# Batch 0's way through the setup of a fused 16-batch layer kernel: order of the first loads, q and k by halves of the heads, and who packs when

## The reference

```python
# 0: adapter with an expert chosen by domain_id, residual, layer norm
h = gelu(x @ down_W.T + down_b); h = (h @ expert_W[id].T + expert_b[id]) + domain_emb[id]
x = ln(h @ up_W.T + up_b + x) * gamma0 + beta0
# 1: attention, 16 heads of 16, modulated by the time step
scale, shift = split(silu(sin_emb(step)) @ W_ada + b_ada)
x1 = ln(x) * (1 + scale) + shift
s = (x1 @ Wq + bq) @ (x1 @ Wk + bk).T / 4 + attention_bias[b, h]      # per head
x = x1 + softmax(where(mask, -inf, s)) @ (x1 @ Wv + bv) @ Wo + bo
x = x + gelu2((ln(x) * g2 + beta2) @ W1 + b1) @ W2
# 2: one of three small networks by condition, residual, layer norm
# 3: finite differences of x times two grids, one time step, relu
```

## Time and profile before

| | |
|---|---|
| three runs | 863.94, 866.76, 868.88 us |
| profiled execution | 864.66 us, span 862.8 us |
| PE busy | 808.2 us (94%), 5968 matmuls |
| DVE, ACT, POOL busy | 738.2 (86%), 622.8 (72%), 164.7 us (19%) |
| TensorE's granted clock | 0.979 of full over the span |
| DMA | 137.33 MB, mean 159 GB/s; queue q1 (SP) 63.4% of 16 engines' span, q10 (ACT) 0.5% |
| chain that ended last | PE 83%, DVE 8%, SPq 3%, ACT 2% |
| side<-in_side | 128 DMAs of 512 KB, median 5.3 us to landing |

### The profile page before, as it was taken

How to read it: one execution, slowest core, us unless ns; L and a number is a source line. 1 busy time by engine, 2 the same in 40 slices (tenths; PEclk the granted TensorE clock), 3 DMA queues, 4 the chain that set the end, 5 groups by cost and what they waited for, 6 DMA issues and landing times.

```text
span 862.8 us, 18592 instructions
## 1 busy us (share of the span) xinstructions
PE 808.2 (94%) x5968; PEld 691.2 (80%) x5968; DVE 738.2 (86%) x2474; ACT 622.8 (72%) x1284; POOL 164.7 (19%) x160
## 2 busy tenths in 40 slices
PE   5686899999999999999999999999999999999992
PEld 2474598888888888888888888888888888887782
DVE  4766777898989899898989898998989898979687
ACT  2445787878778787878788787878788787677541
POOL 3210113030211222030211222030211222111020
PEclk9789999999999999999999999999999999999997
DMA  5866877575866777585767676585777758584100
GB/s 174 232 173 160 212 153 191 143 189 155 175 164 164 185 173 170 139 194 154 176 161 169 178 175 184 123 194 155 174 161 177 181 153 184 130 160 129 58 24 25
DMA packets 147609, 137.33 MB, mean 159 GB/s; under 512 B 19298, under 2 KB 144803, under 8 KB 147508
## 3 DMA queue, kind: packets, MB, share of 16 engines
q1 hardware_dynamic: 146548, 135.28, 63.4%
q10 hardware_dynamic: 960, 0.79, 0.5%
HBM read 98.23 MB, written 4.23 MB: 119 GB/s over the span
## 4 chain that ended last, share of the span: by engine, by line
PE 83%; DVE 8%; SPq 3%; issue 2%; ACT 2%; DMA 1%; ACTq 1%; POOL 0%; DVEq 0%; POOLq 0%
PE back_bank L1366 13%; PE turn_bank L1322 12%; PE context_bank L1376 7%; PE score_bank L1562 7%; PE score_bank L1563 6%; PE front_bank L1360 5%; PE attend_bank L1360 5%; PE back_bank L1360 5%; PE front_bank L1415 3%; PE back_bank L1346 3%; PE back_bank L1337 3%; PE attend_bank L1346 3%; PE front_bank L1668 2%; PE attend_bank L1307 2%; PE front_bank L1406 2%
## 5 line engine op out<-in xcount | busy, mean ns | idle before, releaser
L567 ACT ACTIVATE sc<-sc,negmax 128x256 f32<-128x256 f32 x512 | 231.3, 504 | 17.9 <-DVE negmax L1198 16.9
L1198 DVE CUSTOM_DVE_ANT_0 sc<-score_bank,side 128x256 f32<-128x256 f32 x512 | 195.2, 418 | 32.1 <-PE score_bank L1563 26.7
L561 ACT ACTIVATE pt<-turn_bank 128x512 f32<-128x512 f32 x176 | 106.2, 604 | 132.3 <-PE turn_bank L1322 106.6
L1322 PE MATMUL turn_bank<-ident,sc 128*128 128x128 f32 x1024 | 156.9, 276 | 1.1 <-ACT sc L567 1.0
L1322 PEld LDWEIGHTS turn_bank<-ident,sc 128*128 128x128 f32 x1024 | 123.5, 141 | 31.9 <-issue 14.1
L1562 PE MATMUL score_bank<-ks,qs 128*128 128x256 f32 x512 | 122.5, 321 | 4.3 <-issue 4.1
L1366 PE MATMUL back_bank<-w,ffT 128*128 128x256 f32 x512 | 118.5, 379 | 0.4 <-DVE ffT L1107 0.4
L1366 PEld LDWEIGHTS back_bank<-w,ffT 128*128 128x128 f32 x512 | 96.7, 190 | 13.5 <-DVE ffT L1107 1.0
L487 POOL TENSOR_TENSOR rstd<-var,half_neg 128x2 f32<-128x2 f32 x64 | 50.9, 796 | 285.8 <-DVE var L960 284.4
L1563 PE MATMUL score_bank<-mask_neg,ident_r 128*128 128x512 f32 x256 | 102.3, 400 | 0.0
L1562 PEld LDWEIGHTS score_bank<-ks,qs 128*128 128x128 f32 x512 | 78.2, 192 | 12.3 <-issue 10.9
(11 more groups left out here) (246 smaller groups left out, 1977.5 us busy)
## 6 DMA issues: line engine op xcount, KB each, us to landing
side<-in_side SPq DMA_DIRECT2D x128, 512.0 KB, 5.3
qs<-qh SPq DMA_DIRECT2D x128, 64.0 KB, 4.2
qs<-ql SPq DMA_DIRECT2D x128, 64.0 KB, 4.2
ks<-kl SPq DMA_DIRECT2D x124, 64.0 KB, 4.3
ks<-kh SPq DMA_DIRECT2D x120, 64.0 KB, 4.0
wb<-in_wb SPq DMA_DIRECT2D x15, 512.0 KB, 7.3
xN<-in_x SPq DMA_DIRECT2D x16, 256.0 KB, 4.6
wc<-in_wc SPq DMA_DIRECT2D x16, 256.0 KB, 2.9
```

The costliest lines, as they stand in the source:

```text
L561: e.activation(pt[:, h % NP2, :, :], two(tbank[h % 2]), ACT.Copy).then_inc(copied[h % 4], 1)
L567: i = e.activation(sc[:, h % NS, q, :], sc[:, h % NS, q, :], ACT.Exp, bias=negmax[:, q, h:h + 1], scale=-1.0)
L1198: i = e.tensor_tensor_reduce(sc[:, s % NS, q, :], two(sbank[s % 2])[:, q, :], side[:, (H * X.i + s) % NSIDE, q, :], -1.0, 3.4e38, ALU.add, ...
L1322: i = e.transpose(tbank[h % 2][:, k * S + q * P:k * S + q * P + P], sc[:, h % NS, q, k * P:k * P + P], ident[:, :])
```

## The change

First loads: SP issues the domain ids and x first; ScalarE issues step and kind ids, freq and dt, which count to other semaphores. w_ada, b_ada and wq go out ahead of the expert. w1, bo and wo move behind x of batch 1, the mask and the first side tiles, together with the grids; the ada rows are stored from within that list. d1T, d2T, b2, gamma3 and beta3 move from (-1, 1) to (0, 3). x and expert of batch 2 are loaded at (-1, 8), ahead of the second half's packing, instead of in slot 0 of turn 0. In turn -1 q and k are projected by halves: half 0 of q into `tbank[0]`, of k into `tbank[1]`, half 1 of q into `sbank[1]`, of k into `fbank`. ScalarE and DVE take their high and low parts one half after the other. Packing of half 0 in turn -1 is split, q on SP and k on ScalarE. The ada rows are written by ScalarE. Scaling of w1 follows v on ScalarE, its low part moves to slots 3 and 5 of turn 0 on DVE, the matmuls for b1 from slot 3 to 2. ScalarE packs batch 1's k two DMAs per slot in slots 9 to 12.

```diff
         @block.sync
-            for k in range(3):
-                e.dma_start(ids[:, k, :], ...).then_inc(ld_ids, 16)
-            e.dma_start(dt, d["dt"].partition_broadcast(P)).then_inc(ld_ids, 16)
-            load(ld_ids, (freq, ...))
+            load(ld_ids, (ids[:, 0, :], d["dom"].partition_broadcast(P)))
             load(ld_x, (xN[:, :, :], ...))
...
-            load(ld_ada_w, (w_ada, blocks(d["w_ada"])))
+            load(ld_ada_w, (w_ada, blocks(d["w_ada"])), (b_ada, ...), (pt[:, 0, :, :], blocks(d["wq"])))
             e.wait_ge(dve_set, IDS_SET)
...
+            def load_early():
+                load(ld_w1, (w1_raw, blocks(d["w1"])))
+                load(ld_bo, (bo[:, :], ...), (wo[:, :, :], blocks(d["wo"])))
+                load(ld_grid, (t_a[:, :, :], ...), (t_b[:, :, :], ...), (t_c[:, :, :], ...))
+                e.wait_ge(act_set, ROWS_SET)
+                e.dma_start(d["ada_rows"], x3T[0:NB, :, :]).then_inc(st_ada, 16)
+                load(ld_grid, (x2[:, :, :], ...), (x3[:, :, :], ...))
+            def load_rows():
                 load(ld_late, (t_u[:, :, :], blocks(d["d1T"])), (t_r2[:, :, :], blocks(d["d2T"])),
                      (b2r[:, :], ...), (gamma3[:, :], ...), (beta3[:, :], ...))
-            later = {(-1, 1): load_grids, (0, 7): ...}
+            later = {(-1, 1): load_early, (0, 3): load_rows, (0, 7): ...}
...
-                    if s == 0 and G and not is_step(t, s, -2, 0):
+                    if s == 0 and G and t not in (-2, 0):
+                        load_x(G)
...
+                    if t == -1 and s == 5:
+                        e.wait_ge(st_ada, 16)
+                        load_ada(G)
+                    if t == -1 and s == 6:
+                        for ready, n, blocks_ in ((act_set, QH0_SET, (0, 1)), (dve_set, QL0_SET, (2, 3))):
+                            e.wait_ge(ready, n)
+                            for b in blocks_:
+                                for u in range(2):
+                                    pack_q(e, 0, b, u)
+                    if t == -1 and s == 8:
+                        load_x(phase(t, 3))
+                    if t == -1 and s == 9:
+                        e.wait_ge(ev["ql_ready"], F.n)
+                        e.wait_ge(ev["kl_ready"], F.n)
...
+                                pack_k(e, 1, b, u)
+                                pack_q(e, 1, b, u)
         @block.gpsimd
-            e.wait_ge(dve_set, IDS_SET)
+            e.wait_ge(ev["wexp_ready"], 1)
             e.memset(vp[:, :, :, :, :], 0.0).then_inc(pool_set, 1)
         @block.scalar
+            for k in (1, 2):
+                e.dma_start(ids[:, k, :], ...).then_inc(ld_ids, 16)
+            e.dma_start(freq, ...).then_inc(ld_l0, 16)
+            e.dma_start(dt, ...).then_inc(ld_l0, 16)
...
+                    if is_step(t, s, -1, 6):
+                        e.wait_ge(dve_set, KEY_SET)
+                        e.wait_ge(pe_set, Q0_DONE)
+                        e.activation(qh[:, 0, :], tbank[0][:, 0:S], ACT.Identity, bias=bq[:, 0:1]).then_inc(act_set, 1)
+                        e.wait_ge(pe_set, K0_DONE)
+                        e.activation(kh[:, 0, :], tbank[1][:, 0:S], ACT.Identity, bias=bk[:, 0:1]).then_inc(act_set, 1)
+                        e.wait_ge(pool_set, KS_SET)
+                        for ready, n, blocks_ in ((act_set, KH0_SET, (0, 2)), (dve_set, KL0_SET, (1, 3))):
+                            e.wait_ge(ready, n)
+                            for b in blocks_:
+                                for u in range(2):
+                                    pack_k(e, 0, b, u)
...
-                        if t == 0:
...
-                            for b in range(NBLK):
-                                for u in range(2):
-                                    pack_k(e, 0, b, u)
+                        if t == -1:
+                            e.wait_ge(ld_w1, 16)
+                            for k in range(KT):
+                                e.activation(w1[:, k, :], w1_raw[:, k, :], ACT.Copy, scale=g2c[:, k:k + 1]).then_inc(act_set, 1)
...
+                    if t == 0 and s in (9, 10, 11, 12):
...
+                        for u in range(2):
+                            pack_k(e, 0, s - 9, u)
         @block.vector
-            e.wait_ge(ld_ids, 5 * 16)
+            e.wait_ge(ld_ids, 3 * 16)
             link(e.tensor_copy(idf[:, :, :], ids[:, :, :]))
+            # ids_ok's three steps and IDS_SET here, the flags behind them
...
+            e.wait_ge(ld_l0, 6 * 16)
...
+            def first_heads():
+                link(e.tensor_copy(wv[:, :, :], th[:, 0, :, :]))
+                e.wait_ge(act_set, QH0_SET)
+                # ql half 0, then KH0_SET: kl half 0, expert_done: g1,
+                # q_done: qh half 1, k_done: kh half 1, then ql and kl half 1
...
-                    for t0, s0, setup in ((-2, 14, set_high_q), (-1, 2, set_first_ada), (-1, 3, set_low_q), (-1, 6, set_rest), ...
+                    for t0, s0, setup in ((-2, 9, set_query), (-2, 10, set_high_key), (-1, 3, set_low_key), (-1, 6, first_heads),
+                                          (-1, 7, set_low_value), (-1, 11, set_output_bias), (0, 3, lambda: set_first_low(0)), ...
         @block.tensor
+                    if is_step(t, s, 0, 2):
+                        e.wait_ge(dve_set, KL0_SET)
+                        e.wait_ge(ev["xa_ready"], 2)
                         e.wait_ge(ld_w1, 16)
...
                             e.wait_ge(ev["x1T_ready"], times(F, 2))
-                            project_T_parts(fbank, wq, wql, 0, x1h, x1l, KT, ev["q_done"])
-                        if t == -1:
-                            expert(G, bbank)
+                            if t == -1:
+                                e.wait_ge(dve_set, QUERY_SET)
+                                project_T_parts(tbank[0], wq, wql, 0, x1h, x1l, 1, pe_set)
+                                e.wait_ge(dve_set, KEY_SET)
+                                project_T_parts(tbank[1], wk, wkl, 0, x1h, x1l, 1, pe_set)
+                                expert(G, bbank)
+                                project_T_parts(sbank[1], wq, wql, 0, x1h, x1l, KT, ev["q_done"], 1)
+                                project_T_parts(fbank, wk, wkl, 0, x1h, x1l, KT, ev["k_done"], 1)
```

More of the change, by code:

```diff
@@ L337, in _ @@
                  (upT[0:A, :], d["upT"]), (upT[ONE:ONE + 1, :], d["up_b"].rearrange("(a n) -> a n", a=1)))
-            load(ld_ada_w, (w_ada, blocks(d["w_ada"])))
+            load(ld_ada_w, (w_ada, blocks(d["w_ada"])), (b_ada, d["b_ada"].rearrange("(a k n) -> a k n", a=1, k=2)),
+                 (pt[:, 0, :, :], blocks(d["wq"])))
             e.wait_ge(dve_set, IDS_SET)
@@ L366, in load_wa @@
                 load(ld_late, (wa[:, :, :], blocks(d["wa"])))
-            later = {(-1, 1): load_grids, (0, 7): lambda: load_w2(0), (0, 11): lambda: load_w2(1), (0, 15): load_wa}
+            later = {(-1, 1): load_early, (0, 3): load_rows, (0, 7): lambda: load_w2(0), (0, 11): lambda: load_w2(1), (0, 15): load_wa}
             def load_side(x, c):
@@ L379, in load_ada, with load_x @@
                 e.dma_start(ada[:, :, :].rearrange("p a n -> p (a n)"), d["ada_rows"][bass.ds(x.i, 1)].rearrange("b n -> (b n)").partition_broadcast(P)).then_inc(ld_ada, 16)
+            def load_x(x):
+                wait(e, ev["xa_ready"], x.p)
+                e.dma_start(xN[:, :, :], d["x"][bass.ds(x.i, 1)].rearrange("b (t p) n -> p (b t) n", p=P)).then_inc(ld_x, 16)
+                wait(e, ev["wexp_ready"], x.p)
+                dom = e.value_load(ids_ok[0:1, 0, bass.ds(x.i, 1)], min_val=0, max_val=NE - 1)
+                e.dma_start(wexp_raw[:, :], d["expert"][bass.ds(dom, 1)].rearrange("e a n -> (e a) n")).then_inc(ld_exp, 16)
             def stack(x, prev, m, blocks):
@@ L541, in bring_gelu @@
                 e.activation(switch[:, :], ident[:, 0:1], ACT.Gelu)
+            for k in (1, 2):
+                e.dma_start(ids[:, k, :], d[("dom", "step", "kind")[k]].partition_broadcast(P)).then_inc(ld_ids, 16)
+            e.dma_start(freq, d["freq"].rearrange("(p a) -> p a", a=1)).then_inc(ld_l0, 16)
+            e.dma_start(dt, d["dt"].partition_broadcast(P)).then_inc(ld_l0, 16)
             e.wait_ge(pool_set, IDENT_SET)
@@ L675, in body @@
                 for s in range(SLOTS):
[L676 to L681, removed]
                     if is_step(t, s, 1, 5):
@@ L830, in _ @@
             e.wait_ge(pool_set, 5)
-            e.memset(cbank[:, :], 0.0).then_inc(dve_set, 1)
-            e.tensor_copy(ident_r[:, :], ident[:, :]).then_inc(dve_set, 1)
             A0, A1, B0, B1, B2 = x2, x3, t_a, t_b, t_c
@@ L882, in set_value_bias, with set_low_value @@
+            def set_low_value():
+                e.tensor_tensor(wvl[:, :, :], th[:, 0, :, :], wv[:, :, :].bitcast(F32), ALU.subtract).then_inc(dve_set, 1)
+                e.wait_ge(dve_set, PROJ_SET)
+                set_value_bias()
+                e.memset(cbank[:, :], 0.0).then_inc(dve_set, 1)
```

(14 more changed lines are left out.)

178 lines of the change are left out of this document (82 added, 96 removed).

## The result

The changed kernel takes 860.85 us (median of 7 runs, 859.46 to 862.85); the kernel before took 864.39 us beside it (7 runs, 863.55 to 868.88). The medians are 3.5 us apart and the means 4.2; the recorded ratio of the two kernels is 0.9937, 95% interval [0.9916, 0.9958], which is 5.4 us (3.6 to 7.3). So it is faster beyond the noise, by well under one per cent. The profiled execution took 859.46 us, span 857.7 us, 5.1 less than before. 861.0 was predicted. Over the later series the runs of the kernel before spread from 863.6 to 869.8 us, many near 864.5 and many near 869; so each kernel is given with its ratio to the runs beside it, and places in profiles, which are of single executions, differ by a microsecond or two without an edit.

What follows compares the result with a forecast made beforehand. Bound: the path from 0 to about 90 us, behind which TensorE alone sets the pace. 3.7 + 2.1 = 5.8 us off the median 866.76 gave 861.0; forecast 859.5 to 862.4 (50%), range 857 to 866.

Steps and rivals of the forecast that it cites:

- 3.7 at v: Turn 0: setup and SP's queue order start v at 63.5 instead of 67.27, 3.7 us earlier.
- 2.1 from the packs: Turn 0, ScalarE: spreading k's packing DMAs over slots saves 2.1 us between v's start and head 12's exp.
- signs of being wrong: Head 8's side tile after 64; SP's waits over 2 us longer; TensorE's unbroken stretch not some 6 us earlier.
- Part 1: Ids, x and first setup: first wexp 1.4 us earlier, first q matmul at about 26.9 instead of 28.31.
- Part 2: Halves of the heads in turn -1: first score at 39.6, 4.7 us earlier; SP's q packs done at 36.6.
- DVE is ready for head 6 at about 54, and is not last there: Turn 0: w1l's 2.47 us on DVE nearly paid by a 2.05 us wait for the expert's weights that goes.
- Part 3: SP's queue to the side tiles: head 6 gains 4.7 us; load_rows gives one back, so v gains 3.7.
- Rival C: SP's queue: load_rows makes head 8 4.3 us later, packs' gain zero, 871.0 us; 9% with another rival's worse half.
- Part 4: ScalarE's packing in turn 0: v's start to head 12's exp 15.4 instead of 17.2 us; 2.1 taken with overlap.
- The upper bound: ScalarE's packing in turn 0: gain of 5.3 us if all four places of two packs are covered.
- Some 10 us later: Turn 1: the target of ScalarE's packs is read only some 10 us after them.

Runs made afterwards that it cites:

- the run with only the spread: Kernel before, with only ScalarE's packing of batch 1's k changed to two DMAs in each of slots 9 to 12: 860.99 us, ratio 0.9903.
- the run with load_rows alone: Changed kernel with only load_rows moved from slot 3 to 5 of turn 0, behind the side tile of heads 8 and 9: 860.37 us, ratio 0.9926.
- the run without the spread: Changed kernel with ScalarE's eight packing DMAs of batch 1's k all in slot 9 of turn 0 again: 864.53 us, ratio 0.9965.

## Why the prediction was right, and where it was not

The total was right (861.0 against 860.85), and that is luck in two ways. The first is that two terms of its sum were wrong in opposite directions. It had 3.7 at v and 2.1 from the packs, 5.8 in all; the profiles have 0.5 and 5.1, less 1.4 given back in turn 1, and 0.9 more in the last turn, 5.1 in all. The second is the base. The 5.8 us were taken from a median of 866.76; the seven runs beside the changed kernel have 864.39, from which the same sum gives 858.6, and the gain between the medians is 3.5.

Two of the prediction's own signs of being wrong came: the side tile of head 8 landed after 64, and turn 1, where TensorE's unbroken stretch begins, started 4.2 us earlier and not some 6.

**Part 1 held.** The cast ended at 6.08 (6.07 said), wexp came at 10.52 (10.4), the first q matmul at 26.72 (26.9). That GpSimd's memset holds DVE is shown now, not only read off: with the memset moved the cast takes 0.19 us, and the casts beside its new place take 4.26. This is the exclusion that the Trainium skill, SBUF — State Buffer, "Who interferes with whom", describes. The memset has to stand beside something. Beside the one short cast it costs 1.0 us, beside wq's casts 2.6 more than vp's memset does there (4.26 against 1.71).

**Part 2: the mechanism right, its end missed.** The store of the ada rows was seen at 32.36 (31 said) and SP was done at 37.91 (36.6), so the first score came 3.6 earlier and not 4.7. What failed is the price of the 32 small matmuls, to which no cost was given: not the slot, since a slot later they cost as much, but their length. They take 3.8 us at a granted clock near 0.95 and 6.8 at 0.50, and in all seven profiles of kernels with the changed setup and b1 in turn 0 they took 6.8. The kernel before had them at 3.77, in a stretch with a granted clock of 0.95, in its profiled execution; the run with only the spread, which has the same code up to there, had them at 6.83, so the length differs between executions. That this makes the spread of the kernel before's runs is a guess, not shown. "DVE is ready for head 6 at about 54, and is not last there" failed too: it was last, with the 2.5 us of w1l in an unbroken queue from 50.45 to 59.8.

**Part 3: the queue as said, the landing not.** Heads 6 and 7's tile went out at 52.10 (51.7 said) and the next, behind load_rows and ada, at 55.62 (55.9). But this tile took 9.4 us, more than the 8.7 that I had as the slowest, and landed at 65.0, after the 64 that I had named as the mark of a wrong prediction. So the tile alone took 3.5 of the 3.7 us, and the lateness of head 2 and DVE took nearly as much once more: DVE and the score were ready only at 64.8. The forecast had taken this tile for the bound of head 8, which the earlier trace rows do not show: in the kernel before it was there at 63.84, and head 8's bias started at 65.32, when DVE came to it without a pause and just behind its score (64.89, 0.39). An earlier tile alone could not move head 8, and in the run with load_rows alone it did not. Two bounds of almost equal height stood at head 8, and undoing one gave nothing (the tile at 59.6: head 8 at 65.47; w1l out of the way: 65.93; b1 out of the way: 66.29), undoing two (tile and w1l, the one pair that was run) brought head 8 1.4 us forward, and all three 3.4 and 4.2 us. Rival C's mechanism, load_rows ahead of the tile, was thus there, with a landing 0.3 us short of the 65.3 from which it would have decided; the gain of part 4, which C had at zero, is what kept the sum. The kernel before at head 8:

```profile
64.89 0.39 PE L1563 MATMUL score_bank<-mask_neg,ident_r 128*128 128x512 f32 x1
64.90 0.42 DVE L922 TENSOR_SCALAR grid_c<-wb 128x512 f32<-128x512 f32 x1
```

**Part 4: right place, wrong mechanism for the larger part, size off by 3.0.** The forecast said that the work on ScalarE's path would not be less and only waits would go. I laid all four places of two issues end to end with ScalarE's work, 5.2 us. In fact an issue and the engine's current instruction run side by side, and only an instruction behind an issue waits: 0.74 + 0.60 us exposed where 4.81 were, so 3.5 of the 5.1 us are issue time that left the path. With that TensorE's down for xT took 1.13 us instead of the 2.07 of the same four matmuls in the run without the spread: there the granted clock was 0.50 from 78.0 to 80.2 us, after a pause of TensorE of 4.38 us, and in the changed kernel it was 1.00 from 72 to 74. The waits of 1.10 and 1.67 us ahead of g0 and of head 12's exp shrank to 0 and 0.73 (head 11's). The upper bound, 5.3 with all four places covered, was the better value. The earlier trace rows could not show it, as nothing of the engine's own stood between the eight issues.

**What turn 1 took back.** "Some 10 us later" was right for k's packs; q's last packs on SP, which the forecast left out, came 1.07 us late.

## What to carry to other kernels

Packing DMAs on ScalarE's queue cost what stands behind them, not what they last: two at a time between longer instructions, eight of them went from 4.8 us to 1.3. Before a gain at the start of a chain is carried down, look for work in the same queue ahead of the next consumer that is moved with it (here b1 and w1l), and price it at the clock that TensorE has there after its pause. And when one wait is removed, read what would be late next: of the three things that held head 8, taking away any one gave nothing.

## What the runs showed of the hardware

- 32 matmuls of one column each: 3.77 us at a granted clock of 0.95 in the profile of the kernel before, 6.83 at 0.50 in the run with only the spread, with the same code up to there; 3.6 to 4.3 in the four runs that have them in turn -1. In the changed kernel, 42.5 to 49.3 us stayed at 0.50 with TensorE busy all the time, after two scores and, before them, a wait of 4.33 us.
- Two packing issues on ScalarE's queue last 1.2 us and run beside a copy or a table load, with 0.74 us exposed behind the copy and nothing behind the table load; eight in a row held the next copy 4.8 us.
- A side tile of 512 KB issued at 55.6 us landed in 9.4 us with five loads (d1T, d2T and three rows) issued in the 3 us before it, and in 4.0 with them behind it; it took 6.9 to 7.1 with them behind it where another side tile went out 1.05 us ahead. The five issues took 2.5 us of the queue.
- DVE's casts of 128x64 elements beside a GpSimd memset of 128x4096: 4.26 us for eight, 0.90 without a memset beside them. One cast of 128x48 int32: 1.21 beside it, 0.19 without.
